# Softplus inside a selective-scan kernel: the max(x, 0) part moved from VectorE to ScalarE, one more addition on GpSimd, and another slot table

## What is computed

```python
u = silu(conv(x_s) + conv_b)
x_dbc = u @ x_proj_w.T                       # dt_raw, B, C
delta = softplus(dt_raw @ dt_proj_w.T + dt_proj_b)
dA = exp(delta * A);  dBu = (delta * u) * B
h = dA_t * h + dBu_t;  y_t = sum_s h * C_t   # a scan over time
y = (y + u * D) * silu(z)
```

## Time and profile before

| what | us |
|---|---|
| three runs | 2661.89, 2669.71, 2659.11 (median 2661.89) |
| the profiled execution, its own time | 2653.93 |
| its span | 2652.2 |
| VectorE busy | 2459.2 |
| TensorE matmuls busy | 2292.8 |
| GpSimd busy | 2031.0 |
| ScalarE busy | 1658.9 |

### The profile page before, as it was taken

One profiled execution on the slowest core, in us unless ns is written; L12 is line 12 of the kernel. 1 busy time (PEld: TensorE's weight loads), 2 busy tenths in 40 slices (PEclk: granted clock), 3 DMA queues, 4 the chain that ended last, 5 costly groups with the idle time before them and its releaser, 6 DMA issues. The chain is left out here.

```text
span 2652.2 us, 47132 instructions
## 1 busy us (share of the span) xinstructions
PE 2292.8 (86%) x14442; PEld 1986.7 (75%) x14442; DVE 2459.2 (93%) x4041; ACT 1658.9 (63%) x4137; POOL 2031.0 (77%) x1607
## 2 busy tenths in 40 slices
PE   3958789899999999998999989999989899998665
PEld 2855578878787887877888877888877787887554
DVE  7679999999999999999999999999999999999997
ACT  3940566666666666666666666666666666666653
POOL 3430678888888888888888888888888888888883
PEclk7858899999999999999999999999999999999776
DMA  7216045565555555555555555555555555542451
GB/s 244 92 40 216 29 124 156 154 176 152 161 151 152 157 160 171 158 157 153 155 160 155 166 163 151 158 156 160 154 162 164 156 152 157 159 113 52 96 100 32
DMA packets 267099, 379.38 MB, mean 143 GB/s; under 512 B 21492, under 2 KB 158324, under 8 KB 266852
## 3 DMA queue, kind: packets, MB, share of 16 engines
q1 hardware_dynamic: 236196, 332.26, 40.2%
q0 software_dynamic: 28480, 43.94, 10.1%
q10 hardware_dynamic: 2176, 0.18, 0.1%
HBM read 332.59 MB, written 52.10 MB: 145 GB/s over the span
## 5 line engine op out<-in xcount | busy, mean ns | idle before, releaser
L475 POOL TENSOR_TENSOR h<-du,bbc 128x512 f32<-128x512 f32 x1024 | 1362.5, 1354 | 505.3 <-PE HT L1305 375.3
L1071 DVE TENSOR_TENSOR_SCAN h<-DA,carry,h 128x256 f32<-128x256 f32 x2048 | 1417.7, 734 | 91.4 <-ACT DA L748 79.0
L748 ACT ACTIVATE DA<-delta,alog 128x256 f32<-128x256 f32 x2048 | 882.6, 468 | 212.2 <-DVE h L1071 200.9
L1305 PE MATMUL HT<-ident,h 128*128 128x128 f32 x4096 | 665.8, 288 | 260.5 <-DVE yT L1082 259.1
L1305 PEld LDWEIGHTS HT<-ident,h 128*128 128x128 f32 x4096 | 496.6, 148 | 416.2 <-issue 375.2
L1082 DVE SCALAR_TENSOR_TENSOR yT<-HT,cT,yT 128x512 f32<-128x512 f32 x960 | 698.5, 728 | 3.1 <-PE HT L1305 3.1
L1354 PE MATMUL G<-xtT,W 128*128 128x128 f32 x2160 | 273.2, 281 | 0.0
L1368 PE MATMUL G<-W,fill 128*128 128x256 f32 x1080 | 271.8, 397 | 0.0
L1361 PE MATMUL G<-xtT,W 128*128 128x128 f32 x2160 | 263.4, 275 | 0.0
L1354 PEld LDWEIGHTS G<-xtT,W 128*128 128x128 f32 x2160 | 261.1, 198 | 0.0
L1361 PEld LDWEIGHTS G<-xtT,W 128*128 128x128 f32 x2160 | 252.2, 192 | 0.0
(11 more groups left out here) (183 smaller groups left out, 2986.6 us busy)
## 6 DMA issues: line engine op xcount, KB each, us to landing
W<-in_w_T_dram SPq DMA_DIRECT2D x405, 512.0 KB, 4.2
bbc<-b_dram SPq DMA_DIRECT2D x256, 256.0 KB, 4.3
xraw<-in_x_dram SPq DMA_DIRECT2D x64, 256.0 KB, 2.7
xn_dram<-W SPq DMA_DIRECT2D x8, 1032.0 KB, 14.0
W<-in_x_dram SPq DMA_DIRECT2D x32, 256.0 KB, 6.7
moe_dram<-fill SPq DMA_DIRECT2D x32, 256.0 KB, 4.0
out_dram<-tmpA SPq DMA_DIRECT2D x32, 256.0 KB, 2.2
out_dram<-moe_dram POOLq DMA_DIRECT2D x32, 256.0 KB, 4.4
```

The lines of the kernel that those rows point to most:

```text
L475: pool.tensor_tensor(h[:, v % RING], du[:, b, 2 * q:2 * q + 2, :], bbc[:, s // 2 % BRING, s % 2, :].unsqueeze(1).to_broadcast([P, 2, T]), ...
L748: i = act.activation(DA[:, v % 2, k, :], delta[:, b, c, :], ACT.Exp, scale=nega[:, c, s:s + 1])
L1071: i = dve.tensor_tensor_scan(h[:, v % RING, k, :], DA[:, v % 2, k, :], h[:, v % RING, k, :], carry[:, b, s, c:c + 1], ALU.mult, ALU.add)
L1305: i = pe.transpose(HT[:, k, c * P:(c + 1) * P], h[:, (2 * s + c // 2) % RING, c % 2, k * P:(k + 1) * P], ident[:, :])
```

## The change

ScalarE gets a new step: per half, one ACTIVATE with Relu from `FA` or `FB` in PSUM into `delta`. VectorE's `relu_ln` is gone. GpSimd gets `add_log`, which adds `lnw` to the correction in `tmpA`; `make_delta` waits for that. The slot table and the stage offsets of the expert tiles are others; an offset can now be a tuple, with one entry per tile of the block.

```diff
-    "oacc": 17, "result": 31,
-    "normalise": 6, ... "xs1": 10,
-    "exp": 22, "ln": 23, "sp0": 24, "sp1": 25, "wm": 23, "corr": 24, "delta": 26, "du": 27, "cT": 25, "copy_cT": 26, "out1": 29
+    "oacc": 17, "result": 30,
+    "normalise": 3, ... "xs1": 9,
+    "exp": 21, "ln": 22, "sp0": 23, "sp1": 24, "wm": 22, "corr": 23, "add_log": 24, "delta": 25, "du": 26, "cT": 24, "copy_cT": 25, "out1": 28
-    XT, XT_COPY, H1, H3, TANH, A2, MULT, Y, YO, SCATTER = 0, 1, 2, 3, 3, 4, 4, 5, 6, 8
+    XT, XT_COPY, H1, H3, TANH, A2, SCATTER = 0, 1, 2, 3, 3, 4, 9
+    MULT, Y, YO = (5, 4, 4, 4, 4), (6, 5, 5, 6, 5), (7, 6, 6, 7, 6)
 # GpSimd
+    def add_log(j, b):
+        pool.wait_ge(s_ln, n + 1)
+        pool.wait_ge(s_corr, n + 1)
+        pool.tensor_tensor(tmpA[:, :, :], tmpA[:, :, :], lnw, ALU.add).then_inc(s_pl, 1)
     def make_delta(j, b):
         pool.wait_ge(s_sp, 2 * n + 2)
-        pool.wait_ge(s_corr, n + 1)
+        pool.wait_ge(s_pl, n + 1)
 # ScalarE
     def halo_in(j, b):
-        wait(act, s_sp, 2 * n)
+        wait(act, s_delta, n)
+    def relu_dt(j, b, q):
+        act.wait_ge(s_dtmm, 2 * n + q + 1)
+        wait(act, s_du, n - 1)
+        act.activation(delta[:, b, 2 * q:2 * q + 2, :], (FA if q else FB)[:, :, :], ACT.Relu).then_inc(s_sp, 1)
 # VectorE
-    def relu_ln(j, b, q):
-        dve.wait_ge(s_ln, n + 1)
-        dve.scalar_tensor_tensor(out=delta[...], in0=(FA if q else FB)[...], scalar=0.0, in1=lnw[...], op0=ALU.max, op1=ALU.add).then_inc(s_sp, 1)
```

More of the change, by code:

```diff
@@ L168, in build @@
          s_route, s_tot, s_cnt, s_slot, s_oh, s_xtr, s_xtT, s_h1, s_h3, s_th, s_a2, s_ha,
-         s_y2, s_yo, s_sc, s_mz, s_add, s_gate, s_iota, s_inv, s_gt, s_ix, s_idx, s_nw, s_bias, s_seed, s_y0) = [sem(n) for n in """
+         s_y2, s_yo, s_sc, s_mz, s_add, s_gate, s_iota, s_inv, s_gt, s_ix, s_idx, s_nw, s_bias, s_seed, s_y0, s_pl) = [sem(n) for n in """
             s_par s_prep s_id s_x s_xres s_xn s_oacc s_tr s_xT s_xsmm s_zmm s_xs s_halo s_conv s_tu
@@ L174, in build @@
             s_route s_tot s_cnt s_slot s_oh s_xtr s_xtT s_h1 s_h3 s_th s_a2 s_ha
-            s_y2 s_yo s_sc s_mz s_add s_gate s_iota s_inv s_gt s_ix s_idx s_nw s_bias s_seed s_y0""".split()]
+            s_y2 s_yo s_sc s_mz s_add s_gate s_iota s_inv s_gt s_ix s_idx s_nw s_bias s_seed s_y0 s_pl""".split()]
         s_w = [sem(f"s_w{i}") for i in range(WSLOTS)]
@@ L240, in tile_of @@
             for k in range(PER):
-                at = U * (k // len(XT_UNITS)) + XT_UNITS[k % len(XT_UNITS)] + stage
+                at = U * (k // len(XT_UNITS)) + XT_UNITS[k % len(XT_UNITS)]
+                at += stage[k % len(XT_UNITS)] if isinstance(stage, tuple) else stage
                 for pair in (0, 1, -1):
@@ L269, in build @@
         SLOTS = {"z0": 31, "tanh_z0": 0, "silu_z0": 1, "z1": 2, "tanh_z1": 3, "silu_z1": 4,
-                 "first0": 3, "first1": 4, "y0": 4, "gate_y0": 6, "y1": 5, "gate_y1": 7, "out0": 27, "out1": 29,
-                 "oacc": 17, "result": 31,
[1 row of a table removed]
+                 "first0": 3, "first1": 4, "y0": 4, "gate_y0": 6, "y1": 5, "gate_y1": 7, "out0": 27, "out1": 28,
+                 "oacc": 17, "result": 30,
[1 row of a table added]
                  "conv0": 11, "conv1": 12, "conv2": 13, "conv3": 14, "tanh_u0": 13, "silu_u0": 14, "tanh_u1": 15, "silu_u1": 16,
[2 rows of a table removed]
[1 row of a table added]
+                 "wm": 22, "corr": 23, "add_log": 24, "delta": 25, "du": 26, "cT": 24, "copy_cT": 25}
         XT_UNITS = (4, 13, 18, 23, 30)
@@ L488, in correction @@
                 pool.tensor_tensor(tmpA[:, :, :], tmpB[:, :, :], tmpA[:, :, :], ALU.subtract).then_inc(s_corr, 1)
+            def add_log(j, b):
+                n = number(j, b)
+                pool.wait_ge(s_ln, n + 1)
+                pool.wait_ge(s_corr, n + 1)
+                pool.tensor_tensor(tmpA[:, :, :], tmpA[:, :, :], lnw, ALU.add).then_inc(s_pl, 1)
             def make_delta(j, b):
@@ L527, in _ @@
             correction(0, 0)
+            add_log(0, 0)
             make_delta(0, 0)
@@ L550, in step @@
                             correction(*nxt)
+                        if due("add_log", v):
+                            add_log(*nxt)
                         if due("delta", v):
@@ L768, in front @@
                 abs_dt(j, b, 1)
+                relu_dt(j, b, 0)
+                relu_dt(j, b, 1)
                 exp_dt(j, b)
@@ L844, in step @@
                             abs_dt(*nxt, 1)
+                        for q in range(2):
+                            if due(f"sp{q}", v):
+                                relu_dt(*nxt, q)
                         if due("exp", v):
@@ L1055, in silu_u @@
                                          in1=(FA if q else FB)[:, :, :], op0=ALU.add, op1=ALU.mult).then_inc(s_u, 1)
-            def relu_ln(j, b, q):
-                n = number(j, b)
-                dve.wait_ge(s_ln, n + 1)
-                dve.scalar_tensor_tensor(out=delta[:, b, 2 * q:2 * q + 2, :], in0=(FA if q else FB)[:, :, :], scalar=0.0,
-                                         in1=lnw[:, 2 * q:2 * q + 2, :], op0=ALU.max, op1=ALU.add).then_inc(s_sp, 1)
             def scan(j, b, v):
@@ L1142, in _ @@
             moments(EARLY * NT, TILES)
-            for q in range(2):
-                relu_ln(0, 0, q)
             refine(EARLY * NT, TILES)
@@ L1172, in step @@
                                 silu_u(*nxt, q)
-                        for q in range(2):
-                            if due(f"sp{q}", v):
-                                relu_ln(*nxt, q)
             run(step)
```

## The result

The changed kernel takes 2771.8 us (median of 4 runs, 2770.2 to 2774.5) against 2664.3 of the kernel before measured with it (4 runs): a ratio of 1.040, 95% interval 1.038 to 1.043. Forecast were 2769, a range of 2715 to 2803, and "slower" with 0.89.

A forecast was written before the change was run, and what follows sets the result against it. VectorE was taken as the bound, with ScalarE showing through at a few units. 27 blocks x (3.9 - 0.1) = 103, plus 8 for edge blocks, gave 111 more: 2765 or 2773 by base, stated as 2769, range 2715 to 2803.

The forecast's parts named there:

- VectorE's 1.2 us: Two instructions removed from VectorE in each block: 1.2 us a block, 38 in 32 blocks.
- The wait at scan 24: VectorE waits 2.2 us for `DA` from ScalarE at scan 24, the exponential being one unit earlier.
- The rival in which the gain arrives: VectorE's removed 1.2 us count in full, 38 us less, 2605 to 2640; chance 6%.
- ScalarE takes it back: Units 21 to 26: ScalarE takes back all that VectorE was given, and 0.73 us more.
- The rival that Relu needs a table of its own: Each Relu brings two table loads of 1.28 us, 5.1 a block on ScalarE, 2850 and more; chance 2%.
- GpSimd's chain: GpSimd's work from the exponential to the next block's first product (unit 0') delays scan 0': 3.9 us longer a block.
- The product ahead of which the wait now stands: `make_dbu` of unit 26 on GpSimd, now behind the wait for the exponential, joins the chain: 1.24 us.
- The scatter: The scatter of tile 1, moved from unit 21 to 22, falls inside GpSimd's chain: 1.15 us.
- The wait at unit 31: VectorE, ready for scan 31 at 25.9, gets GpSimd's product at 28.5: a wait of 2.6 us.
- The other slots: `normalise`, MULT of tile 0 and other moved steps: together -0.1 us a block, with -0.5 and +0.5 as ends.
- The clock: TensorE's clock falls after new idle stretches at units 24 and 31: 14 to 30 us more, 2783 to 2800; chance 14%.
- The edge blocks: Four hand-overs outside the 27 blocks with expert tiles: between 0 and 3.8 us each, taken as 2, so 8.

The follow-up runs named there:

- e7: The changed kernel's division of work (Relu on ScalarE, added addition on GpSimd) with the slot table and offsets of the kernel before: 2716 us, ratio 1.020.
- e8: The kernel before with the new slot table and offsets alone, max(x, 0) and the logarithm's addition still on VectorE: 2725 us, ratio 1.025.
- e6: The changed kernel with each Relu done twice on ScalarE: 2760 us, a single run.
- e1: The changed kernel without the added GpSimd addition; delta gets the logarithm and not the correction: 2697 us.
- e2: The changed kernel with GpSimd's wait for the exponential behind make_dbu of unit 22 in place of ahead of it: 2734 us.
- e3: The changed kernel with the scatter at offset 8 again, so that tile 1's is issued at unit 21, ahead of GpSimd's chain: 2788 us.
- e9: The kernel before with MULT, Y and YO of tile 0 one unit later and the wait for the exponential behind make_dbu: 2694 us, ratio 1.012.
- e11: The kernel before with eight extra products on TensorE in its idle time at units 22 to 23: 2652 us, ratio 0.996.
- e5: The changed kernel with index and gather one unit earlier, the gather of tile 4 issued ahead of du: 2789 us, ratio 1.048.

## Why the prediction was right, and where it was not

**VectorE's 1.2 us do not arrive**: right. The wait at scan 24 was given as 2.2 and is 2.16 in every block with tiles. The rival in which the gain arrives, 6%, is out: e7, the division alone, is 2% slower.

**ScalarE takes it back**: right in place. Relu was bounded by tanh and taken as 0.50 in series and 0.60 by itself; it measured 0.58 to 0.59. The wait at scan 24 does not come from Relu: the sum puts Relu behind that `DA`, and e8, without a Relu on ScalarE, has 1.5 of this wait. That this loss lies inside GpSimd's is shown by e6, where more of it costs nothing. The rival that Relu needs a table of its own is out: the changed kernel's loads ahead of `DA` number 31, as before, and those ahead of the logarithm 32, as before.

```profile
L766 ACT ACT_TABLE_LOAD x31 | 39.8, 1283 | 0.6
```

The Trainium skill (ScalarE: Activation LUTs, Table sets: the hidden batching unit) lists relu in every set, and the trace agrees.

**GpSimd's chain**: right, in kind and in size. Given were 3.9 for the stretch up to scan 0'; from scan 20 on it is 33.9 in all 27 blocks, 4.0 longer than the 30.0 of the 19 undisturbed blocks before. The terms inside were too high, and one piece was missing. `add_log`, 2.40 given, takes 2.14 to the next start (804.12 to 806.26); e7 gives 2.1, and e1's seven shortest stretches 2.3. The product ahead of which the wait now stands, 1.24 given: e2 gives 1.0. The scatter, 1.15 given: e3 gives 0.9, because the scatter of tile 2 then stands ahead of the product of unit 31 in its place. The missing piece is the product right behind a scatter, which takes 1.83 and not 1.27 by itself. In series this is not seen, since the scatter overlaps it, but its end comes later, and with scatter 2 ahead of the product of unit 0' that is why scan 0' waits 1.06 and not 0.75. The wait at unit 31, 2.6 given, is 1.85 on the average. That the terms and the missing piece nearly cancel is luck; how the waits of e2 and e3 pass into one another is not told apart further.

**The other slots**: taken as -0.1 a block, and mis-sized. Ahead of scan 20 an undisturbed block is 0.4 shorter than before (46.4 for 46.8), in the changed kernel and in e8 alike. MULT's wait of 0.5 at unit 8 is gone, as given. `normalise` makes VectorE wait at scan 5 too, but scans 5 and 6 together wait 0.7 in place of 0.6, where I had them 0.5 later. e9 shows what I called nothing: with Y of tile 0 a unit later, xs1 has to be a unit earlier, or 1.0 is lost at unit 14. In this table it is, so the sum was not hurt.

**The clock**: given as a rival of 14% on top of the sum, with no term in the sum, and it is part of the result. After, it costs 0.7 a block ahead of scan 20 (47.1 against 46.4), some 19 us. But I had left out that the kernel before pays it as well, at unit 27: some 0.4 a block (77.2 against 76.8), 11 us. In the changed kernel that place is covered by the chain. The difference is 0.3 x 27 = 8.

**The sum by blocks**: 3.97 for the chain, -0.43 for the slots and 0.28 for the clock make 3.8 (103 us in 27 blocks), where 3.9 and -0.1 had been given. So the step that was mis-sized is the other slots, -0.1 for -0.4, and the clock's 0.3, which had no term, made up for it. That the block came out at 3.8 to the tenth is luck. The bounds of the sum were added up too tight: -32, -14 and -8 against +35, +14 and +8 make 2715 to 2826, not 2725 to 2810; the result lies in both.

**The edge blocks**: 8 given, 16 measured. The last block boundary alone has 8.8 (block 30 takes 80.0 against 71.2), block 0 has 4.1. Block 0 takes 98 in the kernel before and 104 in e11, whose code there is the same, so of the edges I can only say what was measured. This was mis-sized too.

## What to carry to other kernels

An engine with a quarter of its time idle can still have a stretch without slack. Before giving it work, add up its instructions from what starts the stretch to what must be ready at its end, and look at what the new table puts into that stretch besides: here a wait moved ahead of a product (1.0) and a scatter moved by one unit (0.9) cost nearly as much as the added instruction (2.1). Comparing a fixed stretch of every block, as scan 20 to scan 0' here, tells such a chain from what varies elsewhere. And where a wait is made or taken away, look at what TensorE does meanwhile, because its clock can take back more than the wait was worth.

## What the hardware showed that was not expected

- In or behind idle stretches of 1.7 to 3.5 us the granted clock fell from 1.00 to 0.50. While it was down, eight passes of 128x256 took 2.99 to 3.62 in place of 1.89, sixteen of 128x128 up to 3.58 in place of 1.95, four transposes 1.06 in place of 0.60.
- Where in the block the clock is down can repeat from block to block: e3 and e5 have 18 and more blocks of 81.9 in a row, the changed kernel comes back to 80.3, 80.7, 81.5, 81.8 again and again. So a shorter chain (e3) could be slower, and more work on ScalarE (e6) was not slower. That the block's own length sets this is my guess, no run tests it.
- Products that nobody needs, in TensorE's idle 2.25 us, kept the clock up and made the kernel before 0.4% faster (0.2 to 0.65%).
- A GpSimd product right behind a scatter (an indirect DMA issue) was recorded with 1.83 us in place of 1.27, while its start stayed 1.09 behind the scatter's. Behind a gather it was 1.28. What follows the product without a pause is recorded longer too: the added addition 2.72, though the next start is 2.14 behind its own.
